# The state sum ahead of the feed-forward branch's products on TensorE, in a fused vision and text block

## What is computed

```
h = concat([tokens(x), txt]) ; h = h + attn(layernorm(h)) ; h = h + ffn(layernorm(h))

attn: a selective scan over the 274 tokens, once forward and once backward (its own weights each)
  xi, z = split(in_proj(x)) ; xc = silu(causal_conv4(xi)) ; dt, B, C = projections of xc
  state[t] = exp(dt*A) * state[t-1] + (dt*xc)*B        384 channels x 16 states
  y = sum over the 16 states of state*C ; out_proj((y + xc*D) * silu(z))
  layernorm(x + forward + backward)
ffn: layernorm, 12-head attention over 274 tokens, residual, layernorm, MLP of 768, residual
  entries 0 to 15 ("large") with one variant; entries 16 to 31 ("small") with three variants
  of fewer heads and channels, summed with three weights
```

## Time and profile before

| what | value |
|---|---|
| three runs | 5915.49, 5928.38, 5931.79 us |
| profiled execution | 5918.2 us, of which span 5916.4 us |
| DVE busy | 5259.6 us (89%) |
| PE busy | 4785.9 us (81%) |
| ACT busy | 3457.5 us (58%) |
| the 32 steps, from 63.3 to 5731.2 us | 5667.9 us, DVE busy 5216.3 us |
| finish, from 5731.2 us on | 185.2 us, DVE busy 28.9 us |

### The profile page before, as it was taken

How to read it: one execution, slowest core, us unless ns; L and a number is a source line. 1 busy time by engine, 2 the same in 40 slices (tenths; PEclk the granted TensorE clock), 3 DMA queues, 4 the chain that set the end, 5 groups by cost and what they waited for, 6 DMA issues and landing times.

```text
span 5916.4 us, 67241 instructions
## 1 busy us (share of the span) xinstructions
PE 4785.9 (81%) x22624; PEld 3257.5 (55%) x22624; DVE 5259.6 (89%) x4154; ACT 3457.5 (58%) x7266; POOL 1.5 (0%) x9
## 2 busy tenths in 40 slices
PE   5788878877878787888788888888888888888877
PEld 3555555555555555555555555555555655555554
DVE  6999998989999898998999999898998989989971
ACT  3455655555565555665556666566565656656643
POOL 0000000000000000000000000000000000000000
PEclk8888988888889888888889999998999989989985
DMA  3112211212112112112112111112112112111110
GB/s 105 59 44 67 66 41 60 68 38 67 58 43 68 61 45 68 55 47 66 60 45 67 63 45 60 61 45 66 54 47 68 45 60 66 41 61 60 41 32 2
DMA packets 56890, 327.57 MB, mean 55 GB/s; under 512 B 13245, under 2 KB 15741, under 8 KB 23626
## 3 DMA queue, kind: packets, MB, share of 16 engines
q1 hardware_dynamic: 56490, 322.53, 17.3%
HBM read 313.52 MB, written 8.98 MB: 55 GB/s over the span
## 4 chain that ended last, share of the span: by engine, by line
DVE 42%; PE 37%; issue 16%; ACT 4%; DVEq 1%; DMA 0%; SPq 0%; ACTq 0%; POOL 0%; POOLq 0%
DVE hs L993 15%; PE y_ps L426 9%; DVE hs L997 7%; DVE hs L976 5%; PE f_ps L549 4%; DVE neg_max L1100 3%; PE f_ps L597 3%; PE f_ps L505 3%; DVE xc L1056 3%; PE f_ps L522 3%; PE f_ps L608 3%; PE f_ps L496 2%; PE a_ps L474 2%; PE f_ps L562 2%; PE a_ps L464 2%
## 5 line engine op out<-in xcount | busy, mean ns | idle before, releaser
L993 DVE TENSOR_TENSOR_SCAN hs<-decay,hs 128x2192 f32<-128x2192 f32 x384 | 1812.3, 4719 | 19.5 <-DVE decay L983 2.2
L426 PE MATMUL y_ps<-hs,ident 128*128 128x274 f32 x5376 | 1612.7, 433 | 81.9 <-DVE hs L1001 29.5
L736 ACT ACTIVATE decay<-dt,inner_s 128x273 f32<-128x273 f32 x3072 | 1384.7, 517 | 98.7 <-issue 53.1
L426 PEld LDWEIGHTS y_ps<-hs,ident 128*128 128x128 f32 x5376 | 1082.4, 208 | 445.5 <-issue 148.7
L976 DVE TENSOR_TENSOR hs<-b_rows,dtu 128x2192 f32<-128x2192 f32 x384 | 935.6, 2436 | 90.7 <-PE y_ps L426 67.7
L997 DVE TENSOR_TENSOR hs<-hs,c_rows 128x2192 f32<-128x2192 f32 x384 | 935.0, 2435 | 4.5
L549 PE MATMUL f_ps<-ident,hid 92*92 92x92 f32 x3456 | 481.8, 283 | 507.3 <-ACT hid L820 507.3
L549 PEld LDWEIGHTS f_ps<-ident,hid 92*92 92x92 f32 x3456 | 340.9, 141 | 694.1 <-ACT hid L820 616.3
L820 ACT ACTIVATE hid<-f_ps,neg_max 92x274 f32<-92x274 f32 x1152 | 463.3, 481 | 341.3 <-DVE neg_max L1100 341.1
L464 PE MATMUL a_ps<-xn,w_in_s 96*128 96x274 f32 x1536 | 472.9, 435 | 8.9 <-ACT xi L759 5.4
L1100 DVE TENSOR_REDUCE neg_max<-f_ps 92x4 f32<-92x1096 f32 x288 | 370.4, 1286 | 92.2 <-PE f_ps L542 92.0
(11 more groups left out here) (114 smaller groups left out, 5115.3 us busy)
## 6 DMA issues: line engine op xcount, KB each, us to landing
b_rows<-bc_rows SPq DMA_DIRECT2D x128, 1096.0 KB, 5.6
c_rows<-bc_rows SPq DMA_DIRECT2D x128, 1096.0 KB, 5.6
xp<-in_patches SPq DMA_DIRECT2D x32, 588.0 KB, 7.4
out<-h SPq DMA_DIRECT2D x32, 205.5 KB, 2.2
bc_rows<-bc_s SPq DMA_DIRECT2D x64, 34.2 KB, 1.5
h<-in_txt SPq DMA_DIRECT2D x32, 57.8 KB, 2.3
w_in_s<-in_w_in SPq DMA_DIRECT2D x1, 1152.0 KB
fc_s<-in_fc SPq DMA_DIRECT2D x2, 576.0 KB
```

Of the source, the lines that this page charges most:

```text
L426: mm = pe.matmul(y_ps[:, 0:T], ident[:, :], hs[q % 2][:, n, :], start=(q % 2 == 0 and n == 0), stop=(q % 2 == 1 and n == end - 1))
L736: e = act.activation(decay[half][:, n, t], dt[d][:, u, t], ACT.Exp, scale=inner_s[:, d, u, s:s + 1])
L993: dve.tensor_tensor_scan(i, a, i, 0.0, ALU.mult, ALU.add).then_inc(scan_done, 1)
```

## The change

In `step` of PE's program, the state sum of the gap is issued first. It used to stand behind `fine_early` of both entries and behind `fronts_early`. The number of instructions is the same, no semaphore is added or taken away, and the lists of DVE, ACT and SyncE are as before. `finish` has its own order and is not touched.

```
                 for gap in range(GAPS):
-                    for part in endings(d, gap, f, e):
-                        fine_early(*part)
-                    fronts_early(b, d, a, gap)
                     q = d * 6 + gap // 3 - 1
                     if q >= 0:
                         ysum_part(b, q, gap % 3)
                     elif not first(b):
                         ysum_part(ago(b, 1), SCANS - 1, gap % 3)
+                    for part in endings(d, gap, f, e):
+                        fine_early(*part)
+                    fronts_early(b, d, a, gap)
                     for part in endings(d, gap, f, e):
                         fine_late(*part)
```

## The result

The changed kernel takes 5945.43 us (median of 20 runs, 5937.32 to 5972.53), the kernel before 5928.58 us beside it (20 runs, 5915.49 to 5944.26). The ratio is 1.0034, with a 95% interval of 1.0025 to 1.0043: slower by about 17 us. I had forecast 120 us, with 5950 us as the low end.

A forecast was written before the change was run, and what follows sets the result against it. DVE, busy for 89% of the span, and its waits were taken to decide the time. Terms of 75 + 15 + 15 + 14 - 6 + 7 = 120 us gave 6038 to 6048 us; forecast 6045 us, range 5950 to 6110 us.

The forecast's parts named there:

- The waits for the state sum: DVE's waits ahead of phase 0 (67.7 us) fall under 15 us, those of `gate_unit` (93.4 us) to about 50.
- The largest term: Gap 10: gate wait 1.04 us and part 1.38 us delay Q and K and the scores, +75 us over 31 steps.
- gap 12: A part between values product and scores makes the row maximum start later: +0.5 us a step, +15 us.
- the slow pace decides: Rival: added parts of gaps 9, 6 and 33 run at 0.46 us a record, 6125 us; chance 0.15.
- The warm price: Gap 9's part priced at 0.23 us a record, since the slow stretch is gone through in either order.
- the price of 1.38 us: Six records of gap 9's part, at the warm pace, added to the chain of gap 10.
- the slow price of 0.46: Microseconds a record in a slow stretch, 2.76 us for a part of 3 planes.
- Gaps 15 to 18: Scores of gap 16 lose 0.6 us, the 0.89 us wait in gap 18 goes: net -6 us over 31 steps.
- Gaps 32 and 33: Four records leave and six enter the chain from centring to variance: +0.46 us a step, +14 us.
- The change does nothing that shows: Rival: gains and losses meet at the lower bound, 5920 to 5935 us; chance 0.04.
- The waits of gap 9 cost only the wait: Rival: gap 9's part is hidden or the slow stretch ends sooner, +55 us, 5983 us; chance 0.17.
- Faster, the head of the turn gaps decides: Rival: state sum waits go, odd gaps' parts fill PE's idle time ahead of turns, about -40 us, 5888 us; chance 0.10.

The follow-up runs named there:

- The run with gap 9 alone: State sum first only in gap 9, all other gaps in the old order, against the kernel before: 5979.78 us, ratio 1.0088.
- the one behind Q and K: Kernel before, with gap 9's state sum moved between Q and K and the projection: 5958.11 us, ratio 1.0053.
- the ten added records: Five matmuls a step that nothing reads, ahead of Q and K in gap 9; alone in the kernel before: 5877.46 us, ratio 0.9925.
- the run of these two gaps alone: State sum first only in gaps 32 and 33, against the kernel before: 5924.75 us, ratio 1.0004.
- the added matmuls: Unread matmuls ahead of gaps 5 (not in small entries), 9, 15 and 32, in both kernels: 5782.86 us before, 5884.64 us changed.
- the first pair: Both kernels with unread matmuls ahead of gaps 5 (small entries too), 9, 15 and 32: 5819.53 us before, 5934.81 us changed.

## Why the prediction was right in direction and wrong in size

**Right.** The waits for the state sum went where the forecast said: phase 0 to zero, `gate_unit` to 33.7 us (about 50 forecast). The largest term held: Q and K stand behind the part and its gate wait, the maximum of gap 10 waits 3.49 and 3.13 us on average (2.7 to 4.3 forecast), +80 us in the traces for 75. The run with gap 9 alone and the one behind Q and K show both pieces of it. That the sum came so near is in part luck: the part took 2.88 us for 1.38, and the products behind it gave 1.06 back. In gap 12 the maximum waits 1.2 us (about 1 forecast).

**The clock.** The part of gap 9 did run at the lower level: 3.08 us at a granted clock of 0.50, twice the warm 1.55. By that the rival "the slow pace decides" would have been right. But Q and K took 0.58 us less than in the earlier trace rows in exchange (1.42 less in the run with gap 9 alone), and the x_proj product's records went from 572 to 427 ns on average. The warm price was taken because the slow stretch has to be gone through in either order. It was gone through in either order, but it was not equally long in PE's work: estimated from the granted clocks as above, 3.4 us before, 2.8 in the run with gap 9 alone and 4.5 in the changed kernel. By the table of the chain the price of 1.38 us lies between the net 1.0 and 1.8 us of the two orders: the reason was right, the size only roughly. Q and K's eight records in the earlier trace rows take 0.43 us each, less than the slow price of 0.46, because they did not run at one level: their granted clock is 0.90 in the first 0.8 us and 0.50 in the 2.6 us behind, and the projection that follows still has 0.50 in its first 0.6 us, then 0.96 and 1.00. Over 3.4 us Q and K had 0.59, after 2.16 us of idleness. With the ten added records ahead of them they have 1.00:

```profile
2486.90:2489.00 2.10, 2.10 (x9) 1.00 0.00 0
```

**The step that failed.** It is the terms "Gaps 15 to 18" (-6 us forecast, -32 in the traces) and "Gaps 32 and 33" (+14 forecast, -20 in the traces): together 60 of the 71 us that the table places. In gap 10 I reckoned that the slow stretch is paid once, by whatever stands first. In the other gaps I did not follow this to its end.

Gaps 15 to 18. Before, the turn of gap 15 was first after 4.68 us of idleness, and DVE's scores hung on it. Now the part is first, at a time when nobody waits for PE, and it takes the slow pace off the turn (1.11 us for 2.07). I wrote that the scores come 1.4 to 1.6 us later and cost 0.6 us. They come 0.3 us later in the large entry above. They cost nothing in large steps and 0.62 us in small ones, which is 9 us in all and not 19. The other half of this miss has nothing to do with the clock: I had the gain from one step's 0.89 us where the mean was 1.07 and 1.47, which makes 39 us and not 28. And 0.6 - 0.89 is -0.29 us, or -9 us, where the prediction has -6.

Gaps 32 and 33. I took the products there at the pace of before. In the whole change the centring product comes at full clock in half of the large steps, and the output projection behind it is fast in all of them, and the two waits of the gap sum to 20 us less than before. In the run of these two gaps alone the pace stayed slow, and the waits rose as forecast.

**What shows that it is the clock.** With the added matmuls in both kernels the change costs 102 us (115 in the first pair). The forecast, worked out from warm records, was 120. Without the added matmuls it costs 17. Put the other way, keeping the clock up gives the kernel before 137 us (ratio 0.9771) but the changed one only 1.0034 - 0.9939 = 0.95%, 56 us. Read so, the change had already taken some 80 us of what the slow clock cost, and paid about 100 us in longer chains. My sum held only the second. In the traces the same shows in the groups by line: slower records of the state sum, faster ones of the turn, Q and K and x_proj. Three things limit this. The pair isn't equally warm, so some 20 of the 102 us are the clock's. The added matmuls also take PE's time and stand in its list, and no run has them where they would keep nothing warm. And half of the miss in gaps 15 to 18 was the reading of one step.

**The rivals.** By its time the nearest was "The change does nothing that shows" (5920 to 5935 us, 10 us off), and after it "The waits of gap 9 cost only the wait" (5983 us). Neither has the mechanism. The part in gap 9 was not hidden, and the first named no term by which gains and losses would meet. "Faster, the head of the turn gaps decides" had the right place for the give-back, the idle time ahead of the turns, and gave it too little.

**What stays open.** Why a large step of the changed kernel has its centring product at one level or the other after equal idle time was not settled, nor why the clock is up from the output projection on in the whole change and not in the run of gaps 32 and 33. Some 32 of the 103 us between forecast and time are in no gap of the table. The moves of gaps 5 and 6, and of 11 and 12, were not run alone. Number and place of the added matmuls were not tuned, and the 20 us that gap 9's matmuls give outside gap 10 are not explained. That the parts of the change don't add (52 and 86 us for 17) limits what any one-part experiment says about the whole.

## What to carry to other kernels

When work is reordered on a TensorE that idles in many short stretches (81% busy here), ask who stands first after each idle stretch: in these traces that one often had the lower clock (Q and K take 4.02 us, at 0.50 in the step shown, in every step of the run where all but gap 9's part is moved, and 2.42 on average behind that part, at 1.00 in the step shown), though not always (the centring product of gap 32 had 1.00 in one large step and 0.55 in the next). Deferrable work there (gaps 15 to 18 alone: -34 us), or work nobody reads (ten records ahead of Q and K: -43 us), can free the chain behind it. But a deferrable piece must not bring a wait of its own into a chain that DVE waits on, so move it to the head only in those gaps where its own reader is the one that is late (here 5, 11, 17 and 32: -90 us), not everywhere (+17 us). And read a repeated wait as a mean over its steps, not from one.

## What the runs showed of the hardware that was not expected

Ten useless records a step (128x192, 1.79 us together), placed before Q and K, made the kernel 43 us faster, and 1936 of them over the kernel 137 us (2.3%). The 1936 raised the mean granted clock from 0.883 to 0.926. An idle stretch of the same 3.22 us ahead of the same product was followed by a granted clock of 1.00 in one step and 0.55 in the next. With all parts of the state sum but that of gap 9 at the head, Q and K took 4.02 us in all 31 steps, at a granted clock of 0.50 in the one shown. And the runs of one and the same kernel spread over 35 us, the slowest of them at the lowest granted clock (5972.53 us at 0.884).
